# Two cross attentions: query unit in chunk 1, its copies over chunks 1 and 2, token copies in chunks 7 and 8

## The reference

```python
x = _layernorm(x + _L0_attn_ref(x, ...))              # self attention, 16 heads
x = _layernorm(x + _L0_xattn_ref(x, ctx_512, ...))    # self attention + MLP, then cross attention + MLP
x = _layernorm(x + _L0_ffn_ref(x, ...))               # linear layer with FP6 quantized operands
x = _layernorm(x + _L1_attn_ref(x, ...))              # state space and hashed memory block
x = _layernorm(x + _L1_xattn_ref(x, ctx_512, ctx_512, ...))  # cross attention, 16 heads, biases
x = _layernorm(x + _L1_ffn_ref(x, ...))               # mixture of experts
```

```python
qh, kh, vh = heads(q @ Wq + bq), heads(ctx @ Wk + bk), heads(ctx @ Wv + bv)
attn = softmax(einsum('bhqd,bhkd->bhqk', qh, kh) * scale)
out = einsum('bhqk,bhkd->bhqd', attn, vh)
```

## Time and profile before

| | us |
|---|---|
| runs of the kernel | 649.39 median of 3 (642.26 to 652.32) |
| profiled execution | 647.96 |
| its span, from the first to the last instruction | 646.2 |

### The profile page before, as it was taken

How to read it: one execution, slowest core, us unless ns; L and a number is a source line. 1 busy time by engine, 2 the same in 40 slices (tenths; PEclk the granted TensorE clock), 3 DMA queues, 4 the chain that set the end, 5 groups by cost and what they waited for, 6 DMA issues and landing times.

```text
span 646.2 us, 19339 instructions
## 1 busy us (share of the span) xinstructions
PE 599.9 (93%) x8518; PEld 419.4 (65%) x8518; DVE 448.3 (69%) x709; ACT 357.5 (55%) x590; POOL 358.4 (55%) x261
## 2 busy tenths in 40 slices
PE   8679898899999999999998989899999999999997
PEld 4466775566766766767775656556666666666764
DVE  3776728687787787785276855687877877978433
ACT  2245663657657657657354335357466476574552
POOL 1572451578888888783210512277776876856400
PEclk9689999999999999999999999999999999999999
DMA  4830015001101101200041001001101012010000
GB/s 165 230 131 2 3 39 175 2 2 40 39 2 39 38 3 39 27 14 2 3 162 37 2 1 38 1 1 41 25 14 39 2 39 39 3 39 2 4 1 14
DMA packets 29871, 24.13 MB, mean 37 GB/s; under 512 B 25716, under 2 KB 25972, under 8 KB 29788
## 3 DMA queue, kind: packets, MB, share of 16 engines
q1 hardware_dynamic: 29788, 22.90, 13.8%
HBM read 13.23 MB, written 0.23 MB: 21 GB/s over the span
## 4 chain that ended last, share of the span: by engine, by line
PE 72%; DVE 12%; ACT 8%; issue 6%; POOL 1%; DMA 1%; DVEq 0%; POOLq 0%; ACTq 0%
PE psum L1136 20%; PE psum L1037 10%; PE psum L1089 6%; PE psum L1082 5%; PE psum L1084 5%; DVE scratch L1275 3%; PE psum L205 3%; PE psum L1021 2%; PE psum L236 1%; PE psum L1043 1%; PE psum L1056 1%; POOL scratch L640 1%; ACT scratch L1236 1%; PE psum L1050 1%; PE psum L241 1%
## 5 line engine op out<-in xcount | busy, mean ns | idle before, releaser
L1260 POOL TENSOR_TENSOR scratch<-scratch 125x896 bf16<-125x896 f32 x136 | 234.3, 1730 | 133.5 <-ACT scratch L1236 133.3
L1236 ACT ACTIVATE scratch<-psum 125x896 f32<-125x896 f32 x192 | 174.2, 916 | 133.3 <-PE psum L1136 133.0
L1275 DVE TENSOR_REDUCE scratch<-psum 128x1 f32<-128x500 f32 x336 | 211.2, 672 | 21.6 <-PE psum L1037 12.0
L1136 PE MATMUL psum<-scratch 128*128 128x448 bf16 (+2 forms) x768 | 174.7, 352 | 0.7 <-ACT scratch L1236 0.5
L1037 PE MATMUL psum<-scratch 128*128 128x500 bf16 x336 | 126.7, 378 | 7.9 <-DVE scratch L1275 2.5
L1082 PE MATMUL psum<-tok_high,scratch 125*128 125x65 bf16 x1344 | 106.8, 194 | 0.5 <-issue 0.5
L1084 PE MATMUL psum<-tok,scratch 125*128 125x64 bf16 x1344 | 106.1, 193 | 0.0
L1082 PEld LDWEIGHTS psum<-tok_high,scratch 125*128 125x128 bf16 x1344 | 93.8, 98 | 15.9 <-ACT scratch L1236 1.3
L1136 PEld LDWEIGHTS psum<-scratch 128*128 128x128 bf16 (+2 forms) x768 | 68.9, 97 | 52.7 <-DVE scratch L1286 2.6
L1084 PEld LDWEIGHTS psum<-tok,scratch 125*128 125x128 bf16 x1344 | 88.3, 98 | 16.8
L1260 DVE TENSOR_TENSOR scratch<-scratch 125x896 bf16<-125x896 f32 x56 | 70.1, 1254 | 28.4 <-ACT scratch L1236 28.2
(11 more groups left out here) (324 smaller groups left out, 766.7 us busy)
## 6 DMA issues: line engine op xcount, KB each, us to landing
scratch<-scratch SPq DMA_DIRECT2D x16, 192.0 KB, 2.6
raw<-ctx_dram SPq DMA_DIRECT2D x4, 672.0 KB
w_third<-fifth_dram SPq DMA_DIRECT2D x3, 636.0 KB, 5.4
w_third<-third_dram SPq DMA_DIRECT2D x2, 844.0 KB, 8.4
w_third<-third_dram SPq DMA_DIRECT2D x2, 843.5 KB, 6.8
w_fourth<-fourth_dram SPq DMA_DIRECT2D x3, 542.5 KB, 5.9
w_first<-first_dram SPq DMA_DIRECT2D x1, 996.0 KB, 4.8
w_second<-second_dram SPq DMA_DIRECT2D x1, 834.5 KB, 6.6
```

Source lines behind the costliest of these rows:

```text
L1136: mm = nc.tensor.matmul(bank(S + f, HALF), lhs[0:rows, 128 * c:128 * c + 128], rhs[0:rows, HALF * f:HALF * f + HALF], start=(rows == 128), ...
L1236: nc.scalar.activation(CR["p"][0:CP, n % RING, :].rearrange("p (f n) -> p f n", f=2), psum[0:CP, S:S + 2, 0:HALF], ACT.Exp).then_inc(self. ...
L1260: ops.tensor_tensor(CR["pl"][0:CP, n % RING, :], CR["p"][0:CP, n % RING, :], p_high(n % RING), ALU.subtract).then_inc(done, 1)
L1275: nc.vector.tensor_reduce(mxp[:, r, t:t + 1], bank(B, TB), X_AXIS, ALU.max).then_inc(self.aux_freed, 1)
```

## The change

Three things, all in `Cross`:

- The query unit's place on TensorE is chunk 1 instead of 2, ahead of the sums that run in that chunk. With it move its copies: ScalarE and VectorE now take Q0's part in chunk 1 and Q1's in chunk 2 (`units_of`), each behind the chunk's exp and low part. Before, ScalarE took both behind exp of chunk 2, and VectorE took both ahead of the low part of chunk 2.
- ScalarE copies the high parts of tokens in chunks 7 and 8 instead of 3 and 5.
- A branch for units in chunk 0 goes; no unit stood there.

```diff
             if front:
-                at[2] += [FRONT[0:2]]
+                at[1] += [FRONT[0:2]]
...
+            def units_of(self, b, c):
+
+                units = list(itertools.chain(*self.steps[b][c]))
+                if c in (1, 2):
+                    return [u for u in itertools.chain(*self.steps[b][1]) if u[0] == ("Q", c - 1)]
+                return units
...
             def run_act(self, act):
...
-                    units = list(itertools.chain(*self.steps[b][c]))
-                    if c == 0 and b:
-                        for unit in units:
-                            self.act_unit(act, *unit)
-                        units = []
+                    units = self.units_of(b, c)
...
-                    if c == 3 and 0 < b < BATCH - 1:
+                    if c == 7 and 0 < b < BATCH - 1:
                         self.high_act(act, b + 1, 1)
-                    if c == 5 and b < BATCH - 2:
+                    if c == 8 and b < BATCH - 2:
                         self.high_act(act, b + 2, 0)
...
             def run_dve(self, dve, projected=None):
...
-                    units = [u for u in itertools.chain(*self.steps[b][c]) if not self.on_act(u[0])]
+                    units = [u for u in self.units_of(b, c) if not self.on_act(u[0])]
                     if c == LAG - 1 and b:
                         self.mean(dve, b - 1)
-                    if c != 1:
+                    if c not in (1, 2):
                         for unit in units:
                             self.dve_unit(dve, *unit)
                         units = []
```

## The result

The kernel after takes 645.91 us (median of 20 runs, 638.6 to 647.89), the kernel before 649.12 (median of 20, 642.26 to 652.32). The ratio is 0.9943, 95% interval 0.992 to 0.9966: 3.7 us faster, between 2.2 and 5.2 (the two medians are 3.2 apart). The profiled execution took 645.9 us, its span 643.8.

The account below looks back on a forecast made before the run. TensorE is busy 93% of the span, so an edit pays only where it waits. Second cross -3.4, first +1.3, first batches -1.0 make -3.1 us: from 649.4 to 646.3, range 640.5 to 651.5.

Parts of the forecast that it names:

- The price of the mean: TensorE, chunks 1 and 2: moving the query unit bares the wait for VectorE's mean; loss of 0.39 us per batch.
- The waits in chunk 4: TensorE, chunk 4: waits of the score-maximum units, 1.05 us a batch in the second cross, 0.27 in the first, removed.
- What stays of M0's wait: Chunk 4, second cross: the first score-maximum unit still waits 0.06 to 0.2 us for VectorE's second query low half; taken 0.1.
- the counter-case with a split port: Second cross: if VectorE and GpSimd didn't block each other, chunk 1's low part ends by 470.34; sum 0.6 us better.
- The open order in the first cross: VectorE first: chunk 4's first maximum unit doesn't wait; GpSimd first: it waits 0.2 to 0.35 us; taken 0.1.
- First batches: Batch 0 of each cross: the query unit fills waiting holes; 0 to -1.19 us each, taken -0.5.
- The sum: Second cross -3.4 us, first cross +1.3, two first batches -1.0, last batches 0: together -3.1.
- VectorE as the bound: Rival: VectorE's serial chain delays chunk 4's first maximum unit; decides from 0.36 us, with 1.0 gives 657; chance 0.10.
- The gains cancel: Rival: chunk 4's maximum units still wait 0.5 us in the second cross, ScalarE's copies late; 649.4; chance 0.15.
- The mean hidden as well: Rival: the wait for the mean is hidden, 12 x 0.39 comes back, or batch-0 gains are larger; 641.6; chance 0.07.

Follow-up runs that it names:

- query_behind_sums: The kernel after with the query unit behind the sums of chunk 11 instead of ahead of them, still in chunk 1; 0.993 of before, 645.34 us.
- scores3_first: The kernel after with the scores of chunk 3 ahead of the sums of chunk 0 in batches 1 to 7; 0.9865 of before, 642.15 us.
- tokens_only: The kernel before with only the token copies moved to chunks 7 and 8; 0.9942 of before, 645.99 us.
- split_later: The kernel after with GpSimd's first token split of the second cross in chunk 3 instead of chunk 1; 0.9939 of before, 646.78 us.

## Why the prediction was right

Forecast 646.3 (-3.1), measured 645.91 (-3.7, interval -5.2 to -2.2). That the two times lie 0.4 apart is partly luck: the median of before came out 0.3 lower than the 649.4 that I had added to. What holds the forecast up is the chunks. Point by point:

- **The price of the mean, +0.39 a batch.** Right to 0.01: chunk 2 went from 2.59 to 1.79, the length that the last batch had shown, chunk 1 from 1.40 to 2.59. query_behind_sums and scores3_first show that it is a wait for the mean.
- **The waits in chunk 4, -1.05 and -0.27.** Measured -0.98 and -0.28. M0's wait for the low half behind ScalarE's last query copy and M1's for the mean copies went, as the walk along ScalarE's row had it. tokens_only, where M1's went alone, shows them to be two. The token copies cost nothing in their new place: chunks 7 and 8 still last 2.04.
- **What stays of M0's wait, taken as 0.1.** In the second cross 0.08. low(1) ended 0.95 after GpSimd's subtraction, as forecast; split_later and batch 6 show that the hold is the cause. One reading on the way was wrong: low(1)'s 1.44 in the kernel before was not held by the cast but by GpSimd's low part, which ended at 468.20 (the same 1.44 stands in batch 6 without any cast). The forecast for low(1) didn't use the 1.44; the counter-case with a split port did (its 470.34), and no row supports that figure.
- **The open order in the first cross** (M0 waits 0, or 0.2 to 0.35) fell on the good side, and that was luck: no row decided it. I had taken 0.1 between the two, and this one term is most of the distance between the sum and the trace: +0.22 a batch forecast, +0.12 measured, 0.6 us over six batches. VectorE (here first) and GpSimd in the first cross, batch boundary 1 to 2:

```profile
172.97 1.08 DVE L1263 TENSOR_TENSOR scratch<-scratch 125x896 bf16<-125x896 f32 x1
...
174.50 1.07 DVE L1263 TENSOR_TENSOR scratch<-scratch 125x896 bf16<-125x896 f32 x1
```

```profile
173.13 1.29 POOL L1357 CAST tok<-nrm 125x384 bf16<-125x384 f32 x1
174.50 1.86 POOL L1359 TENSOR_TENSOR tok<-nrm,tok 125x384 bf16<-125x384 f32 x1
```

  low(2) and the subtraction are both recorded at 174.50. low(2) took its free 1.07, and the subtraction took 1.86 instead of 0.92.
- **First batches, -0.5 each.** -0.59 and -0.47. The sizes are right, but the bounds were wide, and the -0.5 was a choice between them. In both crosses chunks 1 and 2 took 0.42 less together, the part of the unit that disappeared in the hole. The rest came otherwise: in the first cross chunk 4 grew from 2.59 to 3.75, because the second low half now stands behind a reduction of 1.74 us (L474), chunk 5 gave that back (3.20 to 2.04), and the last 0.16 came in chunk 8 (2.85 to 2.69), for a reason that stays open. In the second cross chunk 3 grew by 0.66 and chunk 4 shrank by 0.71. I had named none of that.
- **The sum.** Second cross -3.5 (forecast -3.4), first +0.7 (+1.3), first batches -1.1 (-1.0): -3.8 in the trace against a forecast of -3.1.
- **The rivals.** VectorE as the bound: M0 waits 0.08, not 0.36. It was close all the same: scores3_first, where M0's turn comes 0.39 earlier, ran into just that chain. The gains cancel: exp(2) started at 469.57, directly behind the first copies at 469.01 + 0.54 and 0.18 after scores(2) had ended, but chunk 3 still lasted 2.17, so nobody waited for it. The mean hidden as well: no.

What the prediction did not see is that the parts overlap. It credited the removed waits to the query copies and the token copy together (2.0 us earlier in ScalarE's order), where the token copy's 0.41 was enough for M1 and M2. Had it asked for each part alone, it would have found that in batches 1 to 6 of the first cross the move of the query unit only costs, once the token copies are gone.

## What to carry to other kernels

When a unit of work is moved off a place, look for the wait that it covered there; a batch that lacks the unit shows the bare price, here to 0.01 us. Price each part of a change alone as well as together: two parts that remove the same wait don't add, and one of them may bring nothing. To hide a short serial step, put work in front of its user that waits for neither, here the next scores, rather than moving the user's neighbours.

## What the chip showed that I had not expected

- When VectorE's low part (two SBUF inputs, 125x896) and GpSimd's subtraction became ready together, VectorE went first in all five batches of the first cross where it happened (1 to 5), with the two starts recorded at most 0.02 us apart. The subtraction then took 1.86 or 1.87 us instead of 0.92 and ended 0.79 after low(2). A recorded duration on these engines holds the wait for the other: 1.44 for a free 1.07 in the earlier trace rows, and 1.70 in the kernel after. The held instruction did not need its whole free time once the other had ended: low(1) 0.95 of 1.07, the subtraction 0.79 of 0.92. The Trainium skill, "SBUF — State Buffer", section "SBUF: two separate sides", has this as an exclusive lock for a whole instruction, and the trace agrees.
- The code outside the crosses is the same in all kernels, yet took 259.0 to 264.5 us in the profiled executions. In the kernel after, the granted clock was 0.84 in a stretch that ran at 1.00 before. So a difference of 1 to 3 us between two profiled spans says nothing about a change; the lengths of the chunks do.
